# Edge sum of a graph layer: four of seven edge lists gathered by row, and VectorE's repeated operands moved to PSUM

## The reference

```python
xn = layernorm(x)
x = x + segment_sum(edge_weight[:, None] * xn[src], dst) + node_vec1 + linear_attention(xn)
x = x + mixture_of_experts(layernorm(x))       # 8 experts, top 2
```

## Time and profile before

| | |
|---|---|
| median of 3 runs | 2285.66 us (2284.79 to 2289.71) |
| the profiled execution, first to last instruction | 2536.7 us |
| TensorE, VectorE, ScalarE, GpSimd busy in it | 2230.1, 1963.9, 1174.3, 1551.1 us |

### The profile page before, as it was taken

How to read it: one execution, slowest core, us unless ns; L and a number is a source line. 1 busy time by engine, 2 the same in 40 slices (tenths; PEclk the granted TensorE clock), 3 DMA queues, 4 the chain that set the end, 5 groups by cost and what they waited for, 6 DMA issues and landing times. The chain is left out here.

```text
span 2536.7 us, 45539 instructions
## 1 busy us (share of the span) xinstructions
PE 2230.1 (88%) x16549; PEld 1930.5 (76%) x16550; DVE 1963.9 (77%) x3350; ACT 1174.3 (46%) x1696; POOL 1551.1 (61%) x1356
## 2 busy tenths in 40 slices
PE   7987799999999899989988998999989944999993
PEld 4656687777887788778877787778877844999993
DVE  7989888788898788878877897879877757555552
ACT  2236544443444344434443454444322235888772
POOL 4750266666676566666665666666766612778883
PEclk9989999999999899989988999999999977999997
DMA  5532422222223222222222222222244453455555
GB/s 151 150 113 87 123 82 75 76 90 78 74 83 90 73 82 76 88 76 80 76 82 73 83 79 84 78 79 77 82 123 139 136 180 61 79 81 83 82 81 133
DMA packets 160931, 235.90 MB, mean 93 GB/s; under 512 B 54834, under 2 KB 121805, under 8 KB 160490
## 3 DMA queue, kind: packets, MB, share of 16 engines
q0 software_dynamic: 70896, 164.43, 25.4%
q1 hardware_dynamic: 75536, 55.29, 7.9%
q10 hardware_dynamic: 14314, 13.68, 1.6%
HBM read 186.46 MB, written 53.24 MB: 94 GB/s over the span
## 5 line engine op out<-in xcount | busy, mean ns | idle before, releaser
L817 POOL DMA_INDIRECT picked<-xn_dram,place x1029 | 1143.9, 1112 | 721.7 <-PE bank L915 289.8
L1027 ACT COPY stage<-bank 128x512 f32<-128x512 f32 x343 | 201.0, 586 | 796.9 <-remote 477.6
L915 PE MATMUL bank<-picked,pick_w 128*128 128x256 f32 x2058 | 518.4, 389 | 3.3 <-issue 3.3
L915 PEld LDWEIGHTS bank<-picked,pick_w 128*128 128x128 f32 x2058 | 405.7, 197 | 65.8 <-issue 5.2
L911 PE MATMUL bank<-window,stage 128*128 128x256 f32 x1568 | 416.9, 409 | 17.8 <-issue 12.8
L903 PE MATMUL bank<-hot_w,hots 128*128 128x128 bf16 x4116 | 312.0, 225 | 49.1 <-issue 44.8
L911 PEld LDWEIGHTS bank<-window,stage 128*128 128x128 f32 x1568 | 300.4, 202 | 65.1 <-issue 25.6
L1164 DVE TENSOR_TENSOR vals<-hot_t,field_rep 128x1666 bf16<-128x1666 bf16 x200 | 203.7, 1041 | 187.8 <-remote 180.2
L1288 DVE TENSOR_TENSOR hot_w<-hots,cur 128x1536 bf16<-128x1536 bf16 x343 | 328.6, 958 | 11.9
L903 PEld LDWEIGHTS bank<-hot_w,hots 128*128 128x128 bf16 x4116 | 267.1, 101 | 92.5 <-issue 54.5
L911 PE MATMUL bank<-stage 128*128 128x256 f32 x1176 | 315.5, 410 | 11.6 <-issue 10.4
(11 more groups left out here) (253 smaller groups left out, 3414.6 us busy)
## 6 DMA issues: line engine op xcount, KB each, us to landing
picked<-xn_dram,place POOLq DMA_INDIRECT x1029
w<-in_L_ffn_W_dram SPq DMA_DIRECT2D x16, 512.0 KB, 8.9
xn_dram<-xn ACTq DMA_DIRECT2D x49, 128.0 KB, 1.9
xT_dram<-xT ACTq DMA_DIRECT2D x49, 128.0 KB, 2.1
base_dram<-acc SPq DMA_DIRECT2D x7, 896.0 KB
sum_dram<-acc SPq DMA_DIRECT2D x7, 896.0 KB
z_dram<-vals SPq DMA_DIRECT2D x7, 896.0 KB
out_dram<-sum_dram SPq DMA_DIRECT2D x1, 6250.0 KB, 21.8
```

What stands on the lines that cost most here:

```text
L817: pool.indirect_dma_start(out=picked[:, i % SETS * PICK + q, :], out_offset=None, in_=xn_dram, in_offset=bass.IndirectOffsetOnAxis(ap=plac ...
L915: mm = pe.matmul(sum_ps[pp], pick_w[i % SETS][:, q, :], picked[:, i % SETS * PICK + q, :], start=False, stop=(q == PICK - 1))
L1027: act.copy(block_sb[pp].rearrange("p j c -> p (j c)"), banks[pp][:, :]).then_inc(a_copied, 1)
```

## The change

- The constants: `DENSE` becomes 3 and `PICK` 4. The dense lists are now the odd source tiles of a group, the picked ones the even ones; the window's DMA loads 3 tiles instead of 4.
- `REP` becomes 8. `cur` and `cur_w` no longer lie in SBUF but in PSUM, banks 2 and 3, one half of a unit (tiles 0 to 3, tiles 4 to 6) in each, with a single buffer. As ScalarE writes 4-byte words there, `table` holds each value twice side by side, and `take` copies the pair as one word. VectorE reads the same words as 2-byte numbers.
- VectorE's order in a tile: one-hots (`hots`), picked weights (`picks`), weighted one-hots (`weigh`, split off `hots`). The three instructions of `rank` are dealt out between them.
- The mixing stage ahead of the loop uses banks 0, 1, 4, 5 instead of 0 to 3.
- `place` is made by a tensor_scalar with a lower bound of 0.

The core of the diff:

```diff
-REP = 16
+REP = 8
...
-    DENSE, PICK = (GRP + 1) // 2, GRP // 2
+    DENSE, PICK = GRP // 2, (GRP + 1) // 2
...
-        table = [sb(f"table{i}", [P, NB, ROWS], BF16) for i in range(2)]
+        table = [sb(f"table{i}", [P, ROWS, NB, 2], BF16) for i in range(2)]
...
-        cur = [sb(f"cur{i}", [P, BU, ROWS, REP], BF16) for i in range(2)]
-        cur_w = [sb(f"cur_w{i}", [P, BU, PICK, REP]) for i in range(2)]
...
+        CUT = (0, 4, BU)
+        CUR_W = CUT[1] * ROWS * (REP // 2)
+        def cur_words(half):
+            return banks[2 + half][:, 0:(CUT[half + 1] - CUT[half]) * ROWS * (REP // 2)]
+        def cur_w(half):
+            return banks[2 + half][:, CUR_W:CUR_W + (CUT[half + 1] - CUT[half]) * PICK * REP]
+        def cur_of(i):
+            half = 0 if i < CUT[1] else 1
+            return cur_words(half).bitcast(BF16).rearrange("p (i f r) -> p i f r", f=ROWS, r=REP)[:, i - CUT[half], :, :]
...
-                sp.dma_start(window[g % 2][:, :, :], rows[:, 0:GRP:2, :]).then_inc(window_in[g % 2], 16)
+                sp.dma_start(window[g % 2][:, :, :], rows[:, 1:GRP:2, :]).then_inc(window_in[g % 2], 16)
...
+            def take(used, par, k, half):
+                act.wait_ge(w_done, used + 1)
+                act.wait_ge(pick_done, used + 1)
+                a, n = k * BU + CUT[half], CUT[half + 1] - CUT[half]
+                act.copy(cur_w(half).rearrange("p (m r) -> p m r", r=REP),
+                         weight[par][:, a:a + n, :].rearrange("p i q -> p (i q)").unsqueeze(2).broadcast_to([P, n * PICK, REP]))
+                words = table[par][:, :, :, :].rearrange("p f b h -> p (f b h)").bitcast(F32).rearrange("p (f b) -> p b f", b=NB)
+                act.copy(cur_words(half).rearrange("p (i f r) -> p i f r", f=ROWS, r=REP // 2),
+                         words[:, a:a + n, :].unsqueeze(3).broadcast_to([P, n, ROWS, REP // 2])).then_inc(cur_done, 1)
...
-                act.copy(block_sb[pp].rearrange("p j c -> p (j c)"), banks[pp][:, :]).then_inc(a_copied, 1)
+                act.copy(block_sb[pp].rearrange("p j c -> p (j c)"), banks[pp][:, 0:DENSE * P]).then_inc(a_copied, 1)
...
-                    if after and i in (2, 4):
+                    if after and i in (CUT[1] - 1, CUT[2] - 1):
...
                 for i in range(BU):
-                    if i + 1 < BU:
-                        picks(t + i + 1, i + 1, odd)
-                    elif after:
-                        picks(t + BU, 0, 1 - odd)
                     if i == 2:
                         dve.wait_ge(cur_done, 2 * (u + 1))
                     if i + 2 < BU:
-                        hots(t + i + 2, i + 2, odd, t + i + 2 if i + 2 < 3 else t + i + 1)
+                        hots(t + i + 2, i + 2, t + i + 2 if i + 2 < 3 else t + i + 1)
...
+                    if i + 1 < BU:
+                        picks(t + i + 1, i + 1)
+                    elif after:
+                        picks(t + BU, 0)
+                    if more and i == 2:
+                        rank_add(s)
+                    if i + 2 < BU:
+                        weigh(t + i + 2, i + 2)
+                    elif after:
+                        weigh(t + i + 2, i + 2 - BU)
+                    if more and i == 2:
+                        rank_fold(s)
```

More of the change, by code:

```diff
@@ L637, in edge_sum @@
     SETS = 4
-    assert 4 * DENSE * P * 4 == 2 * DENSE * D * 4 and DENSE * P == 512 and SETS * PICK >= BU and 2 * DENSE >= BU
+    assert 4 * DENSE * P * 4 == 2 * DENSE * D * 4 and DENSE * P <= 512 and SETS * PICK >= BU and AHEAD == GRP + 1
     with ExitStack() as ctx:
@@ L671, in edge_sum, with cur_w_of @@
         picked = sb("picked", [P, SETS * PICK, D])
-        stage = sb("stage", [P, 2 * DENSE * D])
+        stage = sb("stage", [P, max(2 * DENSE, BU) * D])
         window = [sb("window0", [P, DENSE, D]), stage[:, 0:DENSE * D].rearrange("p (t d) -> p t d", d=D)]
         block_sb = [stage[:, DENSE * D + i * DENSE * P:DENSE * D + (i + 1) * DENSE * P].rearrange("p (j c) -> p j c", c=P) for i in range(2)]
+        CUT = (0, 4, BU)
+        CUR_W = CUT[1] * ROWS * (REP // 2)
+        assert CUR_W + CUT[1] * PICK * REP <= 512 and CUT[2] - CUT[1] <= CUT[1]
+        def cur_words(half):
[5 more added lines that the diff above has]
+            return cur_words(half).bitcast(BF16).rearrange("p (i f r) -> p i f r", f=ROWS, r=REP)[:, i - CUT[half], :, :]
+        def cur_w_of(i):
+            half = 0 if i < CUT[1] else 1
+            return cur_w(half).rearrange("p (i q r) -> p i q r", q=PICK, r=REP)[:, i - CUT[half], :, :]
         HALF = (NB + 1) // 4 * 2
@@ L678, in edge_sum @@
         before_each = bass.AP(tile_pad, 0, [[2 * WIDE, P], [2, CH // 2], [WIDE, 2], [1, CH]])
+        hot_w = [w[:, :, 0:DENSE, :] for w in hot_w]
         def block_ps(par, j):
@@ L700, in xT_part @@
             return picked[:, i, k * P:(k + 1) * P] if c % 2 else stage[:, i * D + k * P:i * D + (k + 1) * P]
-        mix_ps = [banks[i][:, 0:D] for i in range(4)]
+        mix_ps = [banks[i][:, 0:D] for i in (0, 1, 4, 5)]
         kv_ps = [banks[4][:, c * D:c * D + P + 2] for c in range(2)]
@@ L1000, in unpack @@
                 act.wait_ge(table_made, s + 1)
-                at = table[par][:, :, AT_SRC:ROWS].rearrange("p b (f j) -> p b f j", j=DENSE)
-                act.copy(at[:, :, :, bass.ds(j, 1)].rearrange("p b f a -> p (f a) b"), table_ps).then_inc(unpacked, 1)
+                at = table[par][:, AT_SRC:ROWS, :, :].rearrange("p (f j) b h -> p f j b h", j=DENSE)[:, :, j, :, :]
+                act.copy(at, table_ps.unsqueeze(3).broadcast_to([P, FIELDS, NB, 2])).then_inc(unpacked, 1)
             def unpack_list(s, n, q, par):
                 act.wait_ge(table_made, s + 1)
-                act.copy(table[par][:, :, bass.ds(q, 1)].rearrange("p b a -> p (a b)"), table_ps[:, END, :])
+                act.copy(table[par][:, q, :, :], table_ps[:, END, :].unsqueeze(2).broadcast_to([P, NB, 2]))
                 if later(n):
@@ L1033, in sort @@
                 if s % 2 == 1:
-                    unpack(s - 1, (s - 1) // 2, 0)
+                    unpack_list(s - 1, s // 2, s // 2, 0)
                 elif s > 0:
-                    unpack_list(s - 1, s // 2 - 1, s // 2 - 1, 0)
+                    unpack(s - 1, s // 2 - 1, 0)
                 repeat_ranks(s)
@@ L1044, in begin @@
                 act.wait_ge(listed, 3 * PICK)
-                take(0, 0, 0, 0, 0)
-                take(0, 0, 0, 0, 1)
+                take(0, 0, 0, 0)
+                take(0, 0, 0, 1)
                 evacuate(0, 0)
@@ L1064, in unit @@
                     if more and i == 0:
-                        if odd == par:
+                        if odd != par:
                             unpack(s - 1, q, 1 - par)
@@ L1077, in unit @@
                             act.wait_ge(listed, (g + 2) * 3 * PICK)
-                            take(t, 1 - odd, 1 - par, 0, i // 2 - 1)
+                            take(t + i + 1, 1 - par, 0, i // CUT[1])
                         else:
-                            take(t, 1 - odd, par, k + 1, i // 2 - 1)
+                            take(t + i + 1, par, k + 1, i // CUT[1])
                     if more and i == 3:
@@ L1136, in rank, with rank_add @@
             def rank(s):
+                rank_add(s)
+                rank_fold(s)
+                rank_sum(s)
+            def rank_add(s):
                 dve.wait_ge(ahead_done, 3 * s + 1)
@@ L1140, in rank, with rank_fold, rank_sum @@
                 dve.tensor_tensor(ahead[:, :, 0:CH], ahead[:, :, 0:CH], same[:, :, :], ALU.add).then_inc(ahead_done, 1)
+            def rank_fold(s):
                 dve.wait_ge(ahead_done, 3 * s + 2)
                 dve.tensor_tensor(ahead[:, :, 0:HALF], ahead[:, :, 0:HALF], ahead[:, :, NB + 1 - HALF:NB + 1], ALU.add).then_inc(ahead_done, 1)
+            def rank_sum(s):
                 dve.wait_ge(ahead_done, 3 * s + 3)
@@ L1169, in part @@
                 dve.wait_ge(unpacked, s + 1)
-                bits = table[par][:, :, :].bitcast(U16)
-                both, dst = (bits[:, :, at:at + DENSE][:, :, bass.ds(j, 1)].rearrange("p b a -> p (a b)") for at in (AT_SRC, PICK))
+                both, dst = (table[par][:, at + j, :, :].rearrange("p b h -> p (b h)").bitcast(U16) for at in (AT_SRC, PICK))
                 dve.tensor_scalar(dst, both, 0x7F80, None, ALU.bitwise_and)
@@ L1178, in make_list @@
                 dve.wait_ge(unpacked, s + 1)
-                col = table[par][:, :, :].bitcast(U16)[:, :, bass.ds(q, 1)].rearrange("p b a -> p (a b)")
+                col = table[par][:, q, :, :].rearrange("p b h -> p (b h)").bitcast(U16)
                 dve.tensor_scalar(col, col, P - 1, 0x3F80, ALU.bitwise_and, ALU.bitwise_or)
@@ L1183, in make_list @@
                 dve.wait_ge(listed, 3 * n + 2)
-                dve.tensor_tensor(place[par][:, bass.ds(q, 1), :].rearrange("p a b -> p (a b)"), row[:, :],
-                                  first_row[:, bass.ds(s, 1)].broadcast_to([P, NB]), ALU.add)
```

(45 more changed lines are left out.)

## The result

The changed kernel takes 2578.07 us (median of 4, 2576.01 to 2581.24), the kernel before 2287.26 in the same measurement: ratio 1.1268, 95% interval 1.1252 to 1.1285. That is 291 us slower; the forecast was 255 slower, 2541 us, inside a range of 2390 to 2710.

A forecast was written before the change was run, and what follows sets the result against it. TensorE, VectorE and GpSimd (gathers plus 0.30 us gaps) were taken as full at once. Afterwards max(29.6, 29.5, 36.0) = 36.0 us a unit, 5.2 more; 49 × 5.2 = 255, from the median 2286 to 2541 us, range 2390 to 2710.

The forecast's parts named there:

- The cleaned basis of 2297 us: Recorded span of 2536.7 us without 240 us of TensorE stalls blamed on recording: 49 units of 30.8 us plus 787.8.
- The 787.8 us outside the loop: Span outside the edge loop's gathers, kept unchanged because the sorting ahead changes by a few elements only.
- TensorE 1.2 us less a unit: Fewer `blocks` matmuls (9 for 12) and one dense list swapped for a picked one: unit 30.8 becomes 29.6 us.
- VectorE keeps the 2-byte price in PSUM: hots and hot_w stay at 0.52 ns an element with a PSUM operand; VectorE's unit 28.8 to 29.5 us.
- Rival B: VectorE's prices double with PSUM operands: unit 39.3 us, 417 us more, 2703 us; chance 0.13.
- the upper price of the forecast: VectorE's 4-byte price of 1.12 ns an element applied to hots (1.56 us) and hot_w (1.42 us).
- A gather costs 1.25 us from start to start: GpSimd in the edge loop: 0.95 us plus 0.30 idle behind each; 28 gathers need 35.0 us a unit.
- Rival A: Gathers cost less in timed runs than recorded, so TensorE sets the unit: 29.6 us, 59 us less, 2227; chance 0.18.
- The PSUM operands set GpSimd free: hots, hot_w and pick_w no longer hold gathers up: unit 36.0 us and not 40.0.
- Rival C: PSUM operands free nothing, gathers still blocked: unit 40.0 us, 451 us more, 2737 us; chance 0.04.
- What remains of contention: Gathers' waiting under VectorE's other instructions: unit taken as 36.0 us, between 35.0 (none) and 37.3 (0.08 a gather).
- ScalarE and the single buffer: ScalarE's extra writes lie beside other engines; a late single buffer costs some 1.3 us a unit, hidden behind GpSimd.

The follow-up runs named there:

- e5: The kernel before, unchanged, recorded a second time: span 2278.9 us, time 2280.7 us, one run of each.
- e1: The changed kernel with the split of the lists put back (4 dense, 3 gathered), all else as changed: 2257.13 us, ratio 0.9891 to the kernel before.
- e7: The changed kernel without the third and fourth gather of every tile after the first four, matmuls kept: 2203.56 us, ratio 0.9642 to the kernel before.
- e10: e1 (4 dense, 3 gathered, operands in PSUM) with VectorE's order of before: 2259.59 us, ratio 0.9888 to the kernel before.
- e2: The changed kernel with cur and cur_w in SBUF again, same layout, words and buffers: 2722.1 us, ratio 1.1887 to the kernel before.
- e3: The changed kernel without the fourth gather of every tile after the first four, matmul kept: 2324.72 us, ratio 1.0176 to the kernel before.
- e6: e1 (4 dense, 3 gathered) with cur and cur_w in SBUF: 2346.72 us, ratio 1.0269 to the kernel before.
- e9: e6 (4 dense, 3 gathered, operands in SBUF) with VectorE's order of before: 2289.32 us, ratio 1.0007 to the kernel before.

## Why the prediction was right

The sign and the mechanism are as forecast, the size 36 us short of 291. By its steps:

- **The cleaned basis of 2297 us.** Taking the stalls out was right, though it rested on two clean units and on a sum that fitted; the reason given was half wrong: e5 shows that recording doesn't cause them. The unit before is 30.6 us on average and not 30.8. The 787.8 us outside the loop were kept as they are, and this failed a little: the first gather of the changed kernel starts at 298.8 us, of e5 at 288.0. The fourth list of the first group is that of its seventh tile, the last that is sorted ahead of the loop; this reason is read from the code, and all runs with four lists in the first group start at 297.8 to 300.1, those with three at 287.4 to 291.0.
- **TensorE 1.2 us less a unit.** 30.0 (e1) and 28.8 (e7): the difference is right, both levels were 0.8 too high. The units of 30.8 us that I took for clean still held gaps that the units of e1 don't have. Before, TensorE was at its limit but for 0.6 us a unit; that e10 gains 30 us with less waiting on GpSimd puts these down to GpSimd.
- **VectorE keeps the 2-byte price in PSUM.** hots 813 ns against 817 forecast, hot_w 747 against 758, pick_w 680 against 700. Rival B falls with it. The Trainium skill's page "Vector Engine (DVE) Microarchitecture Reference", §5.1, agrees; the tier table of "VectorE: DVE Perf Modes" does not: at the upper price of the forecast hots would take 1.56 us.
- **A gather costs 1.25 us from start to start.** Right, and the term that decides: 28 × 1.25 = 35.0 of the 36.5 us. Rival A falls with it, since the recorded span (2576.5) and the timed runs (2578.07) agree.
- **The PSUM operands set GpSimd free.** Right: 0.95 us under hots, hot_w and pick_w, and e2 prices it at 144 us. Rival C is out.
- **What remains of contention** was the mis-sized term: 36.0 us a unit was taken between 35.0 and 37.3, and 36.5 was measured, 0.5 us or 24 us over the loop. The unit before (30.6 for 30.8) is 9 more, the later first gather 11. With these the forecast would be 299; the recorded spans of the changed kernel and of e5 differ by 297.6, the timed runs by 291. e3 and e6 show why it can't be sized from shares of time: most gathers wait for the end of one such instruction, as the forecast had it, but some wait through two to six, which makes them up to 4.2 us longer.
- **ScalarE and the single buffer** cost nothing that shows: e9 is equal to the kernel before.

Left open: what caused the stalls of the first recorded execution, and when a gather waits through more than one instruction.

## What to carry to other kernels

Count an engine's gaps as well as its busy time: a gap that is the same after every instruction is a part of its price, and GpSimd at 69% busy was full. Moving work from TensorE to gathers pays only while (gathers a unit) × (duration + gap) stays below the unit; here three of seven lists fit and four don't. The 1% that there was to gain came from the operands in PSUM alone. One operand of VectorE's two-operand instructions in PSUM frees GpSimd, here at no cost to VectorE; where both stay in SBUF, the order of the instructions can matter (57 us here), so look for the longest gathers and not only at their mean.

## What the runs showed of the hardware

- A gather that is held up under VectorE instructions with both operands in SBUF ends 0.82 us after the end of one of them. The Trainium skill, "SBUF — State Buffer", section "SBUF: two separate sides", has the lock held for the whole instruction. Most gathers of e6 agree, some 450 of 507; 60 wait through two to six instructions, the longest for 5.17 us in all.
- A gather of 64 rows takes 0.90 us, one of 128 rows 0.95; of half as many bytes, 0.94 to 0.95. The 0.305 us behind each is the same in all runs.
- A two-operand instruction on 2-byte numbers runs at the same speed with one operand in PSUM: hots 813 ns in PSUM, 825 in SBUF (e2), hot_w 747 and 749.
